# Attention loop on one core: product with the values and output projection one step later, every step's probabilities turned by VectorE through DRAM

## The chip, the cores and the metric

One NeuronCore of one Trainium2 chip. The metric is the device time of one execution in microseconds (us); the runs of the kernel before gave a median of 1366.54 us over three (1366.28 to 1366.75). Lower is better. The engines are called here by the profile's short names: PE is TensorE (PEld its weight loads), DVE is VectorE, ACT is ScalarE, POOL is GpSimd, SP is SyncE, which in this kernel issues all the copies to and from DRAM of the attention loop. Each engine works through its own instructions strictly in program order and is held to the others by semaphores.

## What is computed

Layernorm, cross attention, layernorm, and a mixture of experts with a shared expert, all in float32, over 2048 tokens (32 sequences of 64) of width 512. Only the attention matters here. Cut from the reference:

```
q = rmsnorm(layernorm(x) @ Wq.T, q_norm_w)        # 32 heads of 128
k = rmsnorm(ctx @ Wk.T, k_norm_w)                 # 8 groups of 128, each serves 4 heads
v = ctx @ Wv.T                                    # 8 groups of 128
scores = q @ k.T / sqrt(128) + mask               # 64 x 64 for each sequence and head
out = softmax(scores) @ v
x = x + tanh(g_xattn) * (out @ Wo.T)
```

## The kernel before

The matrix products of float32 data are made of three products of parts: each operand is split in a high part, rounded by ACT, and a low part, the rest, which DVE subtracts; `split_product` (L675 to L679) multiplies high by low, low by high and high by high.

Stage 1 (to about 187 us) makes keys, values and layernormed rows and puts keys and values in DRAM (`kbuf`, `vbuf`). Stage 2 is the attention loop, to about 1040 us. Stage 3 is the mixture of experts and the final sum; the change doesn't touch stages 1 and 3.

The attention loop has STEPS = 64 steps: 8 key groups, and in each NC = 8 steps of 256 tokens (4 sequences). A step has two halves of 128 tokens. What is done for the data of step j, in its order:

- `q_head` (L746) on PE: the queries of two heads per half, 24 matmuls with 512 columns; ACT copies them (`q_out`, L1226, to `qs`) and squares them (`squares`, L1231, to `sq`).
- The sum of the squares: DVE turns the squares by 32x32 blocks and sums them (`turn_squares`, `sum_squares`, `split_sums`), PE finishes the sum with one small matmul (`add_quarters`, L773, into `ps2`), DVE reads it (L1667, L1672), POOL makes the inverse root (`inverse_root`, L566, to `qr`).
- `scores` (L755) on PE, queries by keys (`kt`, one buffer, which holds the keys of two steps): it waits for `kt_in`, that is for the four loads of `load_k` (L363), one of which fills 32 partitions.
- `softmax` (L1656) on DVE, with the exponential on ACT (`exps`): scale, mask, maximum, difference, sum, reciprocal, product. It ends with `p_ready`; the probabilities are in `pb`, one buffer. Into its waits other work is put (`while_root`, `while_exp`).
- The probabilities turned, keys in the partitions. For odd steps: `transpose_probs` (L787) on PE, four transposes, then ACT and DVE split them out of `ps2` and `ps3` (`probs_hi`, `probs_lo`). For even steps 4 to 54 (`BY_DMA`): DVE turns 32x32 blocks (L1738, `pb` to `pbT`, one buffer), SP stores them to DRAM (L419, `pbuf`) and loads them back with blocks exchanged (`probs_back`, L441, four loads to `pt_raw`), and ACT and DVE split `pt_raw` in `pth` and `ptl`.
- `probs_v` (L796) on PE, the product with the values, 24 small matmuls; ACT and DVE split the result (`a_hi_tile`, `a_rest`). POOL splits the values (`split_v`, L570).
- `project_out` (L778) on PE, the output projection, 24 matmuls with 512 columns, in two halves; DVE adds each to the sum in SBUF (`add_out`, L1618).

Within one PE step i (`step`, L843) stand, in this order: the queries of step i + 1, in an odd step the transposes of step i in their midst, the product with the values of step i - 1, the scores of step i + 1, and the output projections behind it (`outputs`, L828): second half of step i - 2, first half of step i - 1. The DVE step (`dve_step`, L1732), the ACT step (`act_step`, L1275) and SP's `next_loads` (L413) follow the same count. In `next_loads` the four loads of `load_k` stand in the odd step i, and there nothing waits ahead of them but `s_done`, which says that the scores that still read `kt` are done:

```
if odd:
    sp.wait_ge(s_done, i + 1)
    load_k(d + 1)
```

The last eight steps (from 56) are written without the turning of the squares and with PE transposes for even steps too. SP's loop over steps 4 to 55 is a hardware loop; the other engines' steps are written out, POOL's are a loop.

## Time and profile before

| | us |
|---|---|
| median of three runs | 1366.54 |
| the profiled execution | 1367.91 |
| its span, first to last instruction | 1366.2 |
| what lies around the span | 1.7 |
| PE busy | 1351.8 (99%) |
| DVE busy | 1041.6 (76%) |
| ACT busy | 505.4 (37%) |
| POOL busy | 359.9 (26%) |

The profiled execution took 1367.91 us and its trace spans 1366.2 us of it; it is 1.4 us (0.1%) above the median of the runs. Busy time counts instructions that compute, not waits. Matmuls are pipelined: each is busy until its result is out, so two that follow each other overlap in the records, and the distance of their starts (0.23 us for 512 columns here) is what one costs, not its duration of 0.39 us. PE is at its granted clock of 2.4 GHz (1.00 in the rows) in all of the loop.

### The profile page before, as it was taken

What the parts mean: (1) busy time and instruction counts of PE and PEld (TensorE: products, weight loads), DVE (VectorE), ACT (ScalarE), POOL (GpSimd) and SP (SyncE); (2) the same over time, 40 slices, a digit from 0 to 9 for tenths busy, and PEclk for the clock granted to TensorE, in tenths of its full rate; (3) what the DMA queues carried; (4) which work ended last, traced back from release to release, by engine and by line L of the source; (5) the groups of instructions that cost most, each with busy time, mean ns of one, the idle gap of its engine ahead of it and who ended that gap; (6) DMA issues with size and microseconds to landing.
All of it is one profiled execution on the core that took longest, in us unless ns stands there. A gap on an engine that the chain in (4) does not pass through costs nothing.

```text
span 1366.2 us, 24589 instructions
## 1 busy us (share of the span) xinstructions
PE 1351.8 (99%) x8473; PEld 1092.8 (80%) x8474; DVE 1041.6 (76%) x2190; ACT 505.4 (37%) x1085; POOL 359.9 (26%) x375
## 2 busy tenths in 40 slices
PE   8999999999999999999999999999999999999998
PEld 7888877888888888888888888888887888777777
DVE  6676668898888888898988888888687655334459
ACT  4233244343434444344334343434344321222242
POOL 1122232212121221212121212122112100467746
PEclk9999999999999999999999999999999999999999
DMA  6766631222122221222121222212222344555548
GB/s 208 248 190 204 187 112 40 59 56 72 50 57 66 62 59 47 76 53 59 50 78 48 59 63 66 55 51 59 55 78 85 132 171 161 193 185 162 168 158 297
DMA packets 178209, 146.13 MB, mean 107 GB/s; under 512 B 77376, under 2 KB 139328, under 8 KB 177856
## 3 DMA queue, kind: packets, MB, share of 16 engines
q1 hardware_dynamic: 170592, 120.17, 29.4%
q0 software_dynamic: 7520, 24.65, 5.4%
q8 instruction: 63, 1.03, 0.3%
q14 instruction: 34, 0.28, 0.1%
HBM read 97.06 MB, written 47.71 MB: 106 GB/s over the span
## 4 chain that ended last, share of the span: by engine, by line
PE 80%; DVE 3%; issue 1%; DMA 0%; ACT 0%; POOL 0%; DVEq 0%; ACTq 0%
PE ps L677 20%; PE ps L679 19%; PE ps L678 19%; PE ps L1071 6%; PE ps L761 5%; PE ps L808 4%; PE ps L1087 3%; PE ps L1066 2%; PE ps L793 1%; DVE acc L2086 1%; DVE acc L2093 1%; PE ps L984 1%; PE ps L816 0%; PE ps L1118 0%; PE ps L769 0%
## 5 line engine op out<-in xcount | busy, mean ns | idle before, releaser
L574 POOL CAST vth<-vt 128x256 fp32r<-128x256 f32 x64 | 25.4, 397 | 538.6 <-PE ps L808 536.6
L1268 ACT CAST ah<-ps 128x256 fp32r<-128x256 f32 x256 | 83.1, 381 | 208.4 <-PE ps L679 202.0
L677 PE MATMUL ps<-hT,w0h 128*128 128x512 f32 x384 | 152.2, 396 | 1.2 <-DVE w0l L1542 1.2
L679 PE MATMUL ps<-hT,w0h 128*128 128x512 f32 x384 | 149.8, 390 | 0.0
L678 PE MATMUL ps<-hT,w0l 128*128 128x512 f32 x384 | 149.6, 390 | 0.0
L568 POOL TENSOR_TENSOR qr<-qv,mhalf 128x8 f32<-128x8 f32 x64 | 105.1, 1642 | 139.2 <-DVE qv L1672 113.5
L1228 ACT ACTIVATE qs<-ps,wqk 128x512 f32<-128x512 f32 x128 | 88.2, 689 | 125.8 <-PE ps L679 125.8
L1623 DVE TENSOR_TENSOR acc<-ps,acc 128x512 f32<-128x512 f32 x128 | 88.0, 687 | 50.5 <-PE ps L679 50.3
L677 PE MATMUL ps<-w0l,ah 128*128 128x512 f32 x256 | 105.9, 414 | 0.0
L1241 ACT ACTIVATE pb<-pb 128x256 f32<-128x256 f32 x128 | 48.3, 419 | 154.4 <-DVE pb L1692 154.4
L677 PE MATMUL ps<-w1l,ah 128*128 128x512 f32 x256 | 105.1, 411 | 0.0
L1629 DVE TENSOR_TENSOR al<-ps,ah 128x256 fp32r<-128x256 f32 x256 | 95.7, 416 | 10.4 <-ACT ah L1268 10.4
L677 PE MATMUL ps<-hT,w1h 128*128 128x512 f32 x256 | 101.2, 395 | 0.0
L679 PE MATMUL ps<-w0h,ah 128*128 128x512 f32 x256 | 100.3, 392 | 0.0
L679 PE MATMUL ps<-w1h,ah 128*128 128x512 f32 x256 | 100.2, 391 | 0.0
L678 PE MATMUL ps<-w1h,al 128*128 128x512 f32 x256 | 99.9, 390 | 0.0
L678 PE MATMUL ps<-w0h,al 128*128 128x512 f32 x256 | 99.9, 390 | 0.0
L679 PE MATMUL ps<-hT,w1h 128*128 128x512 f32 x256 | 99.9, 390 | 0.0
L678 PE MATMUL ps<-hT,w1l 128*128 128x512 f32 x256 | 99.7, 389 | 0.0
L1071 PE MATMUL ps<-wgu,xgT 128*128 x376 | 94.9, 382 | 0.2 <-issue 0.2
L1638 DVE STREAM_TRANSPOSE sqT<-sq 128x512 f32<-128x512 f32 x108 | 75.5, 699 | 20.7 <-ACT sq L1236 20.6
L677 PEld LDWEIGHTS ps<-hT,w0h 128*128 128x128 f32 x384 | 72.1, 188 | 16.7 <-DVE w0l L1542 1.4
(255 smaller groups left out, 3172.8 us busy)
## 6 DMA issues: line engine op xcount, KB each, us to landing
wraw<-in_w_att SPq DMA_DIRECT2D x64, 256.0 KB, 2.7
vbuf<-vo SPq DMA_DIRECT2D x16, 512.0 KB, 3.3
kbuf<-ko SPq DMA_DIRECT2D x16, 512.0 KB, 5.3
kt<-kbuf SPq DMA_DIRECT2D x128, 64.0 KB, 2.2
vt<-vbuf SPq DMA_DIRECT2D x64, 128.0 KB, 2.2
wgu<-in_w_gu SPq DMA_DIRECT2D x4, 2048.0 KB, 7.9
y<-ybuf SPq DMA_DIRECT2D x16, 512.0 KB, 6.9
pbuf<-pbT SPq DMA_DIRECT2D x26, 256.0 KB, 2.0
```

What stands on the lines that cost most here:

```text
L568: pool.tensor_tensor(qr[:], qv[:], mhalf[:, 0:8], ALU.pow).then_inc(q_rt, 1)
L677: pe.matmul(dst, l_hi, r_lo, start=first, stop=False)
L678: pe.matmul(dst, l_lo, r_hi, start=False, stop=False)
L679: return pe.matmul(dst, l_hi, r_hi, start=False, stop=last)
L761: mm = pe.matmul(PS[3][h * S:(h + 1) * S, b * S:(b + 1) * S], qs[:, h, b], kt[:, b, :], start=True, stop=True)
L808: mm = pe.matmul(PS[4 + b2][:, bp * 256:(bp + 1) * 256], vhl[v_part][rows, bp, :], pt[p_part][rows, 2 * part + bp, :], start=(z == 0), sto ...
L1071: mm = pe.matmul(PS[2 + q][:, 0:2 * EI], xgT[q][:, k, :], wgu[:, bass.ds(e, 1), k * 2 * EI:(k + 1) * 2 * EI].rearrange("p a n -> p (a n)") ...
L1228: act.activation(qs[:, h].rearrange("p b s -> p (b s)"), PS[h][:], ACT.Copy, scale=wqk[:, 0:1]).then_inc(q_copy, 1)
L1268: act.copy(ah[:, bp, :, b2, :], pv_view(bp, b2)).then_inc(a_hi, 1)
L1623: dve.tensor_tensor(dst, PS[6 + bp][:], dst, ALU.add).then_inc(acc_done, 1)
L1629: dve.tensor_tensor(al[:, bp, :, b2, :], pv_view(bp, b2), ah[:, bp, :, b2, :], ALU.subtract).then_inc(a_lo, 1)
L1638: dve.transpose(sqT[:].rearrange("p n i -> p (n i)"), sq[:, h].rearrange("p b s -> p (b s)")).then_inc(sq_turned, 1)
```

## The change

The constants `BY_DMA` and `TURNED` move, so that the probabilities of all steps from 2 to 56, odd ones too, are turned by DVE and go through DRAM; PE's transposes remain for steps 0, 1 and 57 to 63. To give the way through DRAM its time, step i of PE now takes the product with the values of step i - 2 (before i - 1), and the output projection behind it the second half of step i - 3 and the first of step i - 2. ACT's and DVE's steps follow, POOL splits the values of step j - 2 ahead of the root of step j, and `catch_up` at step 56 does two steps' products, after which the last steps run as before. SP's order is written anew: probabilities out, keys (odd steps), weights' slice, probabilities back, values. The line numbers in the two kernels differ. The core of the diff:

```
 NC = T // CT
 CB = CT // S
 STEPS = KVH * NC
-BY_DMA = (4, STEPS - NC)
-TURNED = (3, STEPS - NC + 1)
+BY_DMA = (2, STEPS - NC + 1)
+TURNED = (4, STEPS - NC + 1)
...
+        def by_dma(i):
+            return BY_DMA[0] <= i < BY_DMA[1]
+        def pT_before(i):
+            return i if i < BY_DMA[0] else i - (BY_DMA[1] - BY_DMA[0])
+        def att(r):
+            return W[r // NC % 2]
+        def raw_view(x_, odd):
+            return pt[x_][:, :, odd * P:odd * P + P].rearrange("p m (q i) -> p q m i", q=4)
...
+            def load_v(j):
+                sp.wait_ge(v_split, 2 * j)
+                sp.dma_start(vt[:].rearrange("p b t -> p (b t)"), vbuf[j]).then_inc(vt_in, 16)
+            def load_slice(i):
                 sp.wait_ge(w_hi, i + 8)
                 sp.wait_ge(w_lo, i + 8)
                 sp.dma_start(wraw[:], w_att[i + NC]).then_inc(wr_in, 16)
+            def probs_out(i):
+                sp.wait_ge(p_turned, i - BY_DMA[0] + 1)
+                if i > BY_DMA[0]:
+                    sp.wait_ge(p_back, 64 * (i - BY_DMA[0]))
+                sp.dma_start(pbuf, pbT[:].rearrange("p c m i -> p c (m i)")).then_inc(p_out, 16)
+            def probs_back(i):
+                sp.wait_ge(p_out, 16 * (i - BY_DMA[0] + 1))
+                sp.wait_ge(pT_evac, 2 * i)
+                for c in range(4):
+                    sp.dma_start(pt_raw[32 * c:32 * c + 32].rearrange("p q m i -> p q (m i)"),
+                                 p_ld[c]).then_inc(p_back, 16)
+            for i in range(STEPS - NC + 1):
+                if by_dma(i):
+                    probs_out(i)
+                if i % 2:
+                    sp.wait_ge(s_done, i + 1)
+                    load_k(i // 2 + 1)
+                if i == 0:
+                    load_v(1)
+                if i % 2 or not by_dma(i):
+                    load_slice(i)
+                if by_dma(i):
+                    probs_back(i)
+                    load_v(i)
+                if i % 2 == 0 and by_dma(i):
+                    load_slice(i)
+            load_v(STEPS - NC + 1)
...
-            split_v(2)
-            with pool.Fori(3, STEPS - 2) as j:
+            inverse_root(3)
+            with pool.Fori(4, STEPS - NC + 2) as j:
+                split_v(j - 2)
+                inverse_root(j)
+            split_v(STEPS - NC)
+            split_v(STEPS - NC + 1)
+            for j in range(STEPS - NC + 2, STEPS - 2):
                 inverse_root(j)
                 split_v(j)
...
+            def projected_0(r, w_o):
                 pe.wait_ge(a_hi, 4 * r + 6)
                 pe.wait_ge(a_lo, 4 * r + 6)
                 pe.wait_ge(acc_done, 2 * r + 2)
                 project_out(0, w_o, (0, 1, 2, 3))
+            def outputs(r, w_before, w_o, o_ready=None):
+                pe.wait_ge(acc_done, 2 * r + 1)
+                project_out(1, w_before, (0, 1, 2, 3))
+                if o_ready is not None:
+                    pe.wait_ge(w_lo, o_ready)
+                pe.wait_ge(pT_evac, 2 * r + 4)
+                projected_0(r, w_o)
+            def next_query(i):
+                if i % NC == NC - 1:
+                    pe.wait_ge(w_lo, i + 5)
+                for h in range(2):
+                    pe.wait_ge(q_sq, 2 * i + 1 + h)
+                    q_head(h, (i + 1) % 2, (i + 1) % NC // 2, att(i + 1)).then_inc(q_done, 1)
+            def step(i):
+                next_query(i)
+                probs_v(i - 2, i % 2)
+                scores((i + 1) // 2, (i + 1) % 2)
+                pe.wait_ge(acc_done, 2 * (i - 2) + 1)
+                project_out(1, att(i - 3), (0, 1))
+                if i + 1 == TURNED[0]:
+                    pe.wait_ge(const_dve, 6)
+                add_quarters(i + 1)
+                project_out(1, att(i - 3), (2, 3))
+                if i % NC == 2:
+                    pe.wait_ge(w_lo, i + 6)
+                projected_0(i - 2, att(i - 2))
+            def catch_up(i):
+                next_query(i)
+                probs_v(i - 2, 0)
+                scores((i + 1) // 2, (i + 1) % 2)
+                q_sums(i + 1)
+                pe.wait_ge(acc_done, 2 * (i - 2) + 1)
+                project_out(1, att(i - 3), (0, 1, 2, 3))
+                projected_0(i - 2, att(i - 2))
+                probs_v(i - 1, 1)
+                pe.wait_ge(acc_done, 2 * (i - 1) + 1)
+                project_out(1, att(i - 2), (0, 1, 2, 3))
+                projected_0(i - 1, att(i - 1))
...
                 project_out(0, W[0], (0, 1, 2, 3))
-                probs_v(1, 1)
                 pe.wait_ge(s_scaled, 3)
                 pe.wait_ge(ss_turned, 3)
                 scores(1, 1)
-                pe.wait_ge(const_dve, 6)
-                pe.wait_ge(acc_done, 4)
-                transpose_probs(2, 0)
-                outputs(1, W[0], W[0])
-                step(1, 1, 2, W[0], W[0], W[0])
+                q_sums(3)
+            opening()
+            for i in range(3, STEPS - NC):
+                step(i)
+            catch_up(STEPS - NC)
+            for i in range(STEPS - NC + 1, STEPS - 1):
+                last_step(i, o_ready=STEPS if i == STEPS - NC + 1 else None, last=(i == STEPS - 2))
...
+            def probs_hi(i, odd, bank=2):
+                if by_dma(i):
+                    act.wait_ge(p_back, 64 * (i - BY_DMA[0] + 1))
+                    act.wait_ge(pv_done, 2 * i + 2 - 2 * odd)
+                    act.copy(raw_view(0, odd), pt_raw[:]).then_inc(pT_hi, 2)
+            def queries(i):
+                act.wait_ge(s_done, i + 1)
+                for h in range(2):
+                    q_out(h, i + 1)
+                    squares(h, i + 1)
+            def act_step(i):
+                queries(i)
+                a_hi_tile(i - 2, 0)
+                if i % 2:
+                    probs_hi(i - 1, 0)
+                a_hi_tile(i - 2, 1)
+                split_slice(i, att(i + NC), i % NC)
+                if i % 2:
+                    probs_hi(i, 1)
+                exps(i + 1)
+            def act_catch_up(i):
+                queries(i)
+                a_hi_tile(i - 2, 0)
+                a_hi_tile(i - 2, 1)
+                split_slice(i, att(i + NC), i % NC)
+                exps(i + 1)
+                a_hi_tile(i - 1, 0)
+                a_hi_tile(i - 1, 1)
+                probs_hi(i, 0)
...
             def probs_lo(i, odd, bank=2):
-                if odd:
+                if by_dma(i):
+                    dve.wait_ge(pT_hi, 2 * i + 2)
+                    dve.tensor_tensor(raw_view(1, odd), pt_raw[:], raw_view(0, odd), ALU.subtract).then_inc(pT_evac, 2)
...
+            def turn_probs(i):
+                dve.wait_ge(p_ready, 2 * i + 2)
+                if i > BY_DMA[0]:
+                    dve.wait_ge(p_out, 16 * (i - BY_DMA[0]))
+                dve.transpose(pbT[:].rearrange("p c m i -> p (c m i)"),
+                              pb[:].rearrange("p (m z) (h j) -> p (z h) m j", z=2, h=2)).then_inc(p_turned, 1)
+            def dve_step(i):
+                odd = i % 2
+                late = i % 2 == 1 and 3 < i < STEPS - NC - 1
+                turn_probs(i)
+                turn_squares(i + 1, 0)
+                sum_squares(i + 1, 0)
+                if odd:
+                    slice_lo(i - 1, att(i + NC), i % NC - 1)
+                turn_squares(i + 1, 1)
+                sum_squares(i + 1, 1)
+                split_sums(i + 1)
+                a_rest(i - 2, 0)
+                def while_root():
+                    if odd:
+                        probs_lo(i - 1, 0)
+                    elif i > 4:
+                        slice_lo(i - 1, att(i - 1 + NC), (i - 1) % NC)
+                    add_out(2 * i - 3, 1, (2 * i - 5) % NT)
+                    a_rest(i - 2, 1)
+                def while_exp():
+                    add_out(2 * i - 2, 0, (2 * i - 4) % NT)
+                softmax(i + 1, while_root, while_exp, turn_before=i - BY_DMA[0] + 1)
                 if odd:
                     probs_lo(i, 1)
+                    if not late:
+                        slice_lo(i, att(i + NC), i % NC)
+            def dve_catch_up(i):
+                turn_probs(i)
+                a_rest(i - 2, 0)
+                def while_root():
+                    add_out(2 * i - 3, 1, (2 * i - 5) % NT)
+                    a_rest(i - 2, 1)
+                def while_exp():
+                    add_out(2 * i - 2, 0, (2 * i - 4) % NT)
+                softmax(i + 1, while_root, while_exp, turn_before=i - BY_DMA[0] + 1)
+                slice_lo(i, att(i + NC), i % NC)
+                a_rest(i - 1, 0)
+                add_out(2 * i - 1, 1, (2 * i - 3) % NT)
+                a_rest(i - 1, 1)
+                probs_lo(i, 0)
+                add_out(2 * i, 0, (2 * i - 2) % NT)
...
+                turn_probs(2)
+                softmax(3, lambda: None, lambda: None, turn_before=1)
+            opening()
+            for i in range(3, STEPS - NC):
+                dve_step(i)```

How the order on the queues moves. `pbuf`, `pt_raw`, `pbT` are the buffers of the way through DRAM, `kt` the keys, `wraw` a slice of the weights, `vt` the values.

SP, the loads of one odd step before (the last rows of the loop over two steps; the ISA rows make addresses and hold the wait):

```order
L439 DMA vt<-vbuf 128x256
L421 REGISTER_ALU
L365 ISA [waits s_done]
L365 DMA kt<-kbuf 32x16x32
L365 ISA
```

and SP, one odd step of the change:

```order
L430 DMA pbuf<-pbT 128x512 [waits p_back,p_turned]
L369 DMA kt<-kbuf 32x16x32 [waits s_done]
L369 DMA kt<-kbuf 32x16x32 x3
L424 DMA wraw<-in_w_att 128x512 [waits w_lo,w_hi]
L436 DMA pt_raw<-pbuf 32x4x128 [waits pT_evac,p_out]
L436 DMA pt_raw<-pbuf 32x4x128 x3
L419 DMA vt<-vbuf 128x256 [waits v_split]
```

The key loads of an odd step stood behind the values' load of the even step and now stand behind a store that waits for `p_turned`, DVE's turned probabilities of the same odd step.

DVE, the end of one step's softmax and the head of the next step, which is odd, before:

```order
L1701 TENSOR_TENSOR pb<-pb,rc 128x256
L1711 TENSOR_TENSOR ptl<-pt_raw,pth 128x4x4x32 [waits pT_hi]
L1638 STREAM_TRANSPOSE sqT<-sq 128x512 [waits q_sq,sq_sums]
L1707 TENSOR_TENSOR ptl<-ps2,pth 128x2x128 [waits pT_hi]
L1707 TENSOR_TENSOR ptl<-ps3,pth 128x2x128 [waits pT_hi]
L1644 TENSOR_REDUCE sqs<-sqT 128x8x2 [waits sq_turned]
L1720 TENSOR_TENSOR w1l<-wraw,w1h 128x512 [waits w_hi]
```

and of the change:

```order
L1742 TENSOR_TENSOR pb<-pb,rc 128x256
L1775 STREAM_TRANSPOSE pbT<-pb 128x512 [waits p_out,p_ready]
L1679 STREAM_TRANSPOSE sqT<-sq 128x512 [waits q_sq,sq_sums]
L1685 TENSOR_REDUCE sqs<-sqT 128x8x2 [waits sq_turned]
L1759 TENSOR_TENSOR w1l<-wraw,w1h 128x512 [waits w_hi]
```

The turning of the probabilities comes directly behind the softmax's last product; the splitting of even and odd probabilities has moved behind the next reading of `ps2` and behind the next softmax.

PE, in the queries of an odd step before (the four transposes between two heads' parts):

```order
L679 MATMUL ps1<-hT,w0h 128x512
L793 MATMUL ps2<-ident,pb 128x128 [waits p_ready]
L793 MATMUL ps3<-ident,pb 128x128
L793 MATMUL ps2<-ident,pb 128x128 [waits p_ready]
L793 MATMUL ps3<-ident,pb 128x128
L677 MATMUL ps1<-hT,w0h 128x512
```

and the scores in every step of the change, which are as they were:

```order
L777 MATMUL ps3<-kt,qs 64x64 [waits kt_in,q_copy]
L777 MATMUL ps3<-kt,qs 64x64 x15
```

The transposes are gone from the odd steps 3 to 55 and from steps 2 and 56; nothing takes their place on PE.

## Rows read from the trace of the kernel before

**Rows 1.** The page's busy time, share of the span, and instructions, by engine.

```profile
PE 1351.8 (99%) x8473; PEld 1092.8 (80%) x8474; DVE 1041.6 (76%) x2190; ACT 505.4 (37%) x1085; POOL 359.9 (26%) x375
```

**Rows 2.** Stretch 250 to 930 us: busy us of each engine (instructions), PEclk, DMA share, GB/s.

```profile
250.00:930.00 680.00, 680.00 (x4815) 555.18 (x4814) 602.67 (x1315) 271.79 (x630) 140.27 (x153) 1.00 0.23 60
```

**Rows 3.** Waits of PE after 14 us, engine, line, releaser: in total, times, longest us.

```profile
PE ps L761 <- ACT qs L1228: 2.7, 3, 1.0
PE ps L677 <- DVE w0l L1542: 1.2, 1, 1.2
```

**Rows 4.** PE's timeline, steps 23 to 25: start us, us, line, operation, tiles, count.

```profile
508.32 1.15 PE L761 MATMUL ps<-kt,qs 128*64 128x64 f32 x32
509.40 0.50 PE L677 MATMUL ps<-w0l,ah 128*128 128x512 f32 x1
...
510.89 0.19 PE L775 MATMUL ps<-sqs_hl,fold 128*128 128x64 f32 x1
...
515.11 0.39 PE L677 MATMUL ps<-hT,w1h 128*128 128x512 f32 x1
...
520.64 0.38 PE L808 MATMUL ps<-ptl,vth 64*128 64x256 f32 x2
...
521.54 1.15 PE L761 MATMUL ps<-kt,qs 128*64 128x64 f32 x32
...
535.25 1.15 PE L761 MATMUL ps<-kt,qs 128*64 128x64 f32 x32
```

**Rows 5.** DVE's timeline of the same steps.

```profile
506.53 0.76 DVE L1707 TENSOR_TENSOR ptl<-ps,pth 128x256 fp32r<-128x256 f32 x2
...
518.25 0.76 DVE L1701 TENSOR_TENSOR pb<-pb,rc 128x256 f32<-128x256 f32 x2
518.93 0.68 DVE L1720 TENSOR_TENSOR w1l<-wraw,w1h 128x512 fp32r<-128x512 f32 x1
519.53 0.70 DVE L1738 STREAM_TRANSPOSE pbT<-pb 128x512 f32<-128x512 f32 x1
...
523.72 0.19 DVE L1654 TENSOR_TENSOR sqs_hl<-sqs,sqs_hl 128x32 fp32r<-128x32 f32 x1
...
532.15 0.68 DVE L1711 TENSOR_TENSOR ptl<-pt_raw,pth 128x512 fp32r<-128x512 f32 x1
```

**Rows 6.** SP's timeline, the opening's key loads and those for step 26.

```profile
226.21 2.02 SPq L365 DMA_DIRECT2D kt<-kbuf  x4
...
520.36 0.33 SPq L419 DMA_DIRECT2D pbuf<-pbT  x1
...
525.08 1.92 SPq L365 DMA_DIRECT2D kt<-kbuf  x4
```

**Rows 7.** Copies by line, KB each, median us from issue to landing.

```profile
kt<-kbuf SPq DMA_DIRECT2D x128, 64.0 KB, 2.2
...
pbuf<-pbT SPq DMA_DIRECT2D x26, 256.0 KB, 2.0
pt_raw<-pbuf SPq DMA_DIRECT2D x104, 64.0 KB, 1.9
```

**Rows 8.** ACT's timeline, the exponential of step 25.

```profile
529.71 0.76 ACT L1241 ACTIVATE pb<-pb 128x256 f32<-128x256 f32 x2 [2.21 <-DVE pb L1692]
```

**Rows 9.** PE's timeline and windows at the program's start, with PE's clock.

```profile
7.16 0.47 PE L677 MATMUL ps<-w0l,c_hi 128*128 128x512 f32 x1 [1.16 <-DVE w0l L1531]
...
10.03 0.50 PE L677 MATMUL ps<-w0l,c_hi 128*128 128x512 f32 x1 [1.94 <-DVE w0l L1531]
...
10.60:15.00 4.40, 4.40 (x14) 3.45 (x13) 3.23 (x5) 3.10 (x5) 0.00 (x0) 0.61 1.03 415
```

**Rows 10.** PE's timeline, scores of steps 1, 3 and 4.

```profile
202.77 1.15 PE L761 MATMUL ps<-kt,qs 128*64 128x64 f32 x32 [0.98 <-ACT qs L1228]
...
224.34 1.15 PE L761 MATMUL ps<-kt,qs 128*64 128x64 f32 x32
...
238.88 1.15 PE L761 MATMUL ps<-kt,qs 128*64 128x64 f32 x32
```

More of the change, by code:

```diff
@@ L841, in outputs @@
                 project_out(0, w_o, (0, 1, 2, 3))
-            def step(d, odd, pair_q, w_q, w_before, w_o, q_ready=None, o_ready=None, last=False, turn=True):
-                i = 2 * d + odd
-                if q_ready is not None:
-                    pe.wait_ge(w_lo, q_ready)
+            def outputs(r, w_before, w_o, o_ready=None):
[5 more added lines that the diff above has]
+                projected_0(r, w_o)
@@ L869, in step @@
                     transpose_h2(3, 1)
-                dma = turn and by_dma(i, odd)
-                if not odd and not dma:
+                if i % 2 == 0:
                     pe.wait_ge(acc_done, 2 * i)
-                    transpose_probs(i, odd)
-                outputs(i - 1, w_before, w_o, o_ready, turn, dma)
+                    transpose_probs(i, 0)
+                outputs(i - 1, att(i - 2), att(i - 1), o_ready)
             for k in range(KD):
@@ L1284, in act_step @@
                 a_hi_tile(i - 1, 0)
-                if not odd and not by_dma(i, odd):
+                if i % 2 == 0:
                     probs_hi(i, 0)
                 a_hi_tile(i - 1, 1)
-                if by_dma(i, odd) and False:
-                    probs_hi(i, 0, d=d)
-                split_slice(i, w, sl)
-                if by_dma(i, odd):
-                    probs_hi(i, 0, d=d)
+                split_slice(i, W[0], i % NC)
                 exps(i + 1)
-            def act_group(d0, p, t0=0):
-                for t in range(t0, NC // 2):
-                    for odd in range(2):
-                        act_step(d0 + t, odd, W[1 - p], 2 * t + odd)
             act.wait_ge(s_done, 1)
@@ L1751, in dve_step, with dve_last @@
+            def dve_last(i, complete=(None, None)):
+                odd = i % 2
+                if odd:
+                    probs_lo(i, 1)
                 if complete[0] is not None:
```

200 lines of the change are left out of this document (44 added, 156 removed).

## Prediction

> **What bounds the kernel now.** I read the busy times first: PE is busy 99% of the span [rows 1]. The windows by stage show that the attention loop is wholly PE's: 680.0 us of 680 at the full clock, with DVE at 602.7 [rows 2]. The waits confirm it: after 14 us the longest wait of PE is 1.2 us, and none recurs in the loop [rows 3]. So in the loop a matmul taken away is time gained, as long as nothing new makes PE wait. PE's timeline gives the price: the scores of steps 24, 25 and 26 start at 508.32, 521.54 and 535.25 [rows 4]. The first distance is 13.22 us, without transposes in it; the second, 13.71, holds the four transposes of step 25. Four transposes therefore cost PE **0.49 us**. I write S for the start of a step's scores.
>
> **The change part by part.**
>
> *PE's transposes.* They go in the odd steps 3 to 55 and in steps 2 and 56. After the scores of step 4 that is 26 odd steps, 26 x 0.49 = 12.7 us, and 0.5 for step 56. Steps 2 and 3 are in the opening, below.
>
> *DVE.* In an odd step it gains a turning of 0.70 and a split from the loaded copy of 0.68 and loses the pair of 0.76 [rows 5]: 0.62 us more per two steps. Its idle time in the loop is 680 - 602.7 = 77.3 us over 680 / 26.93 = 25.3 pairs, 3.1 us a pair [rows 2]. The pair shrinks by 0.49, so 3.1 - 0.6 - 0.5 = 2.0 us stay: cost nothing, PE's matmuls cover it. Without that cover it would be 0.6 us a pair. The finest margin is `add_quarters`: DVE's split ends at 523.91, and two steps earlier PE's product started 2.57 us after S, which here is 524.11 [rows 4, 5]. The turning before it starts at once behind the softmax, in front of other work that had waited there, and the work moved behind the reading of `ps2` fills DVE's wait for the projection. I take no cost; an upper bound comes with a rival.
>
> *ACT and POOL.* Same instructions, other places; both have more idle than busy time [rows 1]: nothing.
>
> *The later product.* PE's probabilities now have a step more, so the DRAM way of store (2.0 us) and load (1.9 us) [rows 7] is no wait for PE. Instead PE owes one step's product with the values (520.64 to 521.54, 0.9 us) and projection (509.40 to 515.11, 5.7 us) [rows 4] once the loop is full, and pays it at step 56: **+6.6 us**, unless the opening gives it back.
>
> *The key loads, the term that decides.* SP's order of an odd step i is now: store of the turned probabilities of step i, then the four key loads, and these keys are for the scores of step i + 1, in PE's same step i. Before, they were issued at 525.08, some 10 us ahead of the scores at 535.25 [rows 4, 6]. Now the queue of SP stands at the wait for `p_turned`, and behind it wait keys, weights' slice, returned probabilities and values; who waits for the keys is PE, with all that follows. For i = 25: S(25) = 521.54; the softmax's last product leaves DVE at 532.15, where now the turning starts [rows 5]; it ends 0.70 later, 532.85. SP issued the store 0.13 after such an end (520.23 to 520.36) [rows 5, 6]: 532.98. The first key load follows after the store's own 0.33 and a little: 533.36. Four of them, outside SP's hardware loop, took 2.02, so the last starts about 1.69 later [rows 6]: 535.05. It lands after 2.2 [rows 7]: 537.25, and PE starts about 0.1 later, 537.35. Without the wait S(26) would stand at 521.54 + 13.22 = 534.76. The wait is **2.6 us**, once in each odd step. Bounds: with 0.35 between issues and 2.0 to landing, 2.0 us; with the loads delayed behind the store's 256 KB, 3.4 us. I take 2.6, as all its pieces are rows of the same copies. For steps 5 to 55: 26 x 2.6 = 67.6 us. The wait doesn't shorten the next chain, since that starts at S(i + 2), 13.22 us behind.
>
> The Trainium skill has a formula for a copy (DMA: Bandwidth & Descriptors, Anatomy of one DMA): about 2.0 us fixed plus the bytes at 436 GB/s. By it a key load would take 2.15 us, and the wait would be 0.05 smaller, 1.3 us in sum; the trace has 2.0 us for the store of 256 KB, for which the formula gives 2.6, so I keep the rows.
>
> *The opening.* The scores of step 3 move forward by the 0.9 us of a product with the values, 224.34 - 0.9 = 223.44 [rows 10]. The same chain with the key loads, 13.22 + 2.6 = 15.8, puts S(4) at 239.3 against 238.88: +0.4 us. PE has only some 8 us of work there and so stands still for over 7.
>
> *PE's clock.* At the start of the program PE idled for 1.16 and 1.94 us with three matmuls between; behind it the granted clock fell from 2.4 to 1.2 GHz, and the stretch 10.6 to 15.0 has a mean of 0.61 [rows 9]: 4.4 x 0.39 = 1.7 us lost. A gap of 0.98 us in dense work was followed by no fall [rows 10, 2]. The new gap of 2.6 us lies beyond both single gaps, but in dense work. Cost of a fall 0 to 1.7 us; I take a fall after half of the 26 gaps, at 1.5 (part of it passes in a gap): 13 x 1.5 = 19.5 us. After the opening's long gap I count one, 1.7 us.
>
> *The sum*, against the profiled execution's 1367.9: -12.7 - 0.5 + 0.4 + 6.6 + 67.6 + 19.5 + 1.7 = +82.6, so 1450.5. The median of the runs was 1.4 us below that execution: **1449 us**.
>
> **The rivals.**
>
> *The keys wait, but the clock never falls in the loop.* For it: every gap has 26 us of dense matmuls around it, and 1 us gaps did nothing. Against: rows 9. It gives 1449 - 19.5 = 1430 us, chance 0.27.
>
> The Trainium skill's TensorE page (TensorE: Matmul & The Clock Gate, Why this matters for your kernels) speaks for this rival: it warns only of gaps between bursts of matmuls that are longer than mine. By that rule the time is 1430. The fall at the start of this trace, after gaps that were shorter, speaks against reading it so.
>
> *The clock falls after every gap.* 26 x 1.7 = 44.2 in place of 19.5: 1474 us, chance 0.13.
>
> *A second wait, for the returned probabilities of odd steps.* Their loads can't be issued before the even ones are split, behind DVE's reading of `ps2`. From S on: about 4.3 to the first issue, 1.7 to the last, 1.9 to landing [rows 6, 7], 0.6 for ACT's copy: 8.5, where the exponential started at 529.71 - 521.54 = 8.17 [rows 4, 8]. The softmax ends some 0.3 later, inside a margin of about 0.5 before `add_quarters` is late. If landing takes 0.7 longer, PE loses 0.5 per pair: 26 x 0.5 = 13, so 1462 us, chance 0.09.
>
> *The keys come in time* (the other side). One mechanism: the probabilities are turned early enough that the first key load is issued before S(i) + 13.22 - (1.7 + 2.2 + 0.1) = S(i) + 9.2, and my chain has it at S(i) + 11.8. The softmax alone ends at S + 10.6 in the rows, so the order on SP or the wait itself would have to be other than I read it. Then only the transposes count, and filling and emptying the pipeline costs about 3 (0 to 6.6, as the opening's shorter PE work is hidden by DVE or not): 1367.9 - 13.2 + 3 - 1.4 = 1356 us, chance 0.07. About the same time as before, by whatever balance: 0.01.
>
> **How the numbers follow.** The forecast, keys late and a clock that falls after part of the gaps, has 0.43; with the rivals' 0.27, 0.13, 0.09, 0.07 and 0.01 that makes 1. The lower end: no falls, and a wait of 2.0, is 1430 - 15.6 = 1414 us. The upper: a fall after every gap and a wait of 3.0 is 1474 + 10.4 = 1484. What is left out is the case of keys in time and the farther tails. A measurement of this kernel tells about 0.2% from no change, 2.7 us. Faster by more than that: 0.07; within: 0.01; slower: 0.92.
>
> **What would show it.** Right: PE's scores of each odd step (those for even data) wait for the copy to `kt`, 2.0 to 3.4 us, 26 or 27 times, and SP's longest waits are for `pbT`; the scores' distances alternate between 13.2 and about 16 us; no transposes of `pb` on PE between 240 and the last eight steps; PE's mean clock in the loop is below 1.00. PE at 1.00 throughout would show the clock's term wrong; distances of 13.2 us alone, the whole forecast; waits of `add_quarters` for the split sums, that the margin on DVE was smaller than I read it.

## The result, and the profile after

The changed kernel takes **1488.8 us** (1488.2 to 1491.1, 4 runs), the kernel before 1366.4 us (1365.6 to 1366.8, 4 runs) beside it: a ratio of 1.090, 95% interval 1.088 to 1.092. The forecast was 1449, with 1414 to 1484 as its range. So the direction was right and the size was not, and the time lies just above the range.

The busy time by engine, as in [rows 1]:

```profile
PE 1386.6 (93%) x8364; PEld 1119.3 (75%) x8365; DVE 1060.7 (71%) x2186; ACT 505.0 (34%) x1058; POOL 380.1 (26%) x375
```

PE has 109 matmuls fewer and yet 35 us more of busy time, and it idles for 101 us of a span of 1487.3. The window of the loop, with the columns of [rows 2], shows both halves of this: PE stands still for 65 of 680 us, and where it runs its clock is not whole any more.

```profile
250.00:930.00 680.00, 614.67 (x4067) 500.51 (x4065) 537.83 (x1135) 235.04 (x522) 135.89 (x131) 0.94 0.25 68
```

What PE waits for, after 14 us (columns of [rows 3]):

```profile
PE ps L777 <- DMA kt<-kbuf: 85.6, 27, 8.0
PE ps L777 <- ACT qs L1255: 2.7, 3, 1.0
PE ps L693 <- issue: 1.2, 1, 1.2
PE ps L693 <- DVE w0l L1583: 1.2, 1, 1.2
```

The first line is new. One of its 27 waits, 7.96 us, is in the opening; the other 26 are in the odd steps, 77.6 us in total, 3.0 on average (2.50 to 3.54). PE's timeline shows one of them, and what follows (L777 are the scores, the L761 of [rows 4]):

```profile
567.78 1.15 PE L777 MATMUL ps<-kt,qs 128*64 128x64 f32 x32
...
584.48 1.98 PE L777 MATMUL ps<-kt,qs 128*64 128x64 f32 x32 [3.38 <-DMA kt<-kbuf]
586.39 0.80 PE L693 MATMUL ps<-w0l,ah 128*128 128x512 f32 x1
...
588.50 0.48 PE L693 MATMUL ps<-w0l,ah 128*128 128x512 f32 x1
...
599.11 1.15 PE L777 MATMUL ps<-kt,qs 128*64 128x64 f32 x32
```

From 567.78 to 584.48 are 16.70 us, where a step without transposes and without a wait took 13.22. Then the 32 matmuls of the scores take 1.98 us for 1.15, and a product takes 0.80 for 0.48. The windows of the gap and of what follows give the clock (PEclk is the column behind POOL's count):

```profile
578.00:582.50 4.50, 3.10 (x22) 2.27 (x20) 4.09 (x8) 2.98 (x7) 1.12 (x2) 1.00 0.42 99
584.50:586.00 1.50, 1.50 (x29) 1.50 (x30) 0.00 (x0) 0.00 (x0) 0.00 (x0) 0.50 0.00 0
587.90:599.11 11.21, 11.21 (x59) 9.03 (x57) 9.84 (x20) 4.50 (x10) 2.02 (x1) 1.00 0.18 52
```

Behind the gap the granted clock is at 1.2 GHz, and from 587.90 at the latest it is at 2.4 again. In the loop 23 of the 26 gaps have such a fall; seven of these last twice as long. The three without one are the shortest gaps of the loop, 2.50, 2.54 and 2.59 us. Toward the end of the loop one has it and the next has not, which PE's timeline shows by the length of the scores:

```profile
956.99 1.98 PE L777 MATMUL ps<-kt,qs 128*64 128x64 f32 x32 [3.13 <-DMA kt<-kbuf]
973.02 1.15 PE L777 MATMUL ps<-kt,qs 128*64 128x64 f32 x32
988.86 1.15 PE L777 MATMUL ps<-kt,qs 128*64 128x64 f32 x32 [2.54 <-DMA kt<-kbuf]
1002.11 1.15 PE L777 MATMUL ps<-kt,qs 128*64 128x64 f32 x32
```

From 956.99 to 973.02 are 16.03 us, a distance with a long fall; from 988.86 to 1002.11 are 13.25, one without.

**Who holds the keys.** DVE's timeline of step 25, and SP's of the same step (S(25) is 567.78):

```profile
577.78 0.76 DVE L1742 TENSOR_TENSOR pb<-pb,rc 128x256 f32<-128x256 f32 x2
578.58 0.71 DVE L1775 STREAM_TRANSPOSE pbT<-pb 128x512 f32<-128x512 f32 x1
```

```profile
579.32 0.32 SPq L430 DMA_DIRECT2D pbuf<-pbT  x1
579.69 2.10 SPq L369 DMA_DIRECT2D kt<-kbuf  x4
581.88 0.43 SPq L424 DMA_DIRECT2D wraw<-in_w_att  x1
```

The turning begins at S + 10.80, the store goes out 0.03 behind its end, and the four key loads run behind the store, as forecast. In place of the 525.08 of [rows 6], which is 3.54 behind the S of its step, their first is 11.91 behind it. SP's waits from 250 to 1060 us, and the landings:

```profile
SPq L430 <- DVE pbT L1775: 293.0, 52, 7.0
```

```profile
pbuf<-pbT SPq DMA_DIRECT2D x55, 256.0 KB, 2.0
pt_raw<-pbuf SPq DMA_DIRECT2D x220, 64.0 KB, 2.0
kt<-kbuf SPq DMA_DIRECT2D x128, 64.0 KB, 2.4
```

The store lands in 2.0 us as before; the key load takes 2.4 where [rows 7] have 2.2. PE waits for the last of the four, and that one takes 2.6 on average in the odd steps, at most 3.1.

**The account,** from the starts of the scores. S(4) is 239.45, +0.57 to before. From S(4) to S(57) are 826.5 us, before 713.6: +112.9. In it the 26 distances that end at scores of even data grew from 13.71 to a mean of 16.33, which is -0.49 for the transposes, 12.7 us in sum, and +3.11 for the wait (3.0 of it recorded as PE's idle time), 80.7 us in sum; the other 27 grew from 13.22 to a mean of 14.88, 44.9 us in sum, for the clock. From S(57) to S(58) are 22.24 us for 14.53: +7.7. Together +121.1, which is the difference of the two spans, 1487.3 and 1366.2.

### The profile page after: what moved, and what is told of

Its sections match the earlier page's. It is cut to its first block, busy times and chain, and to the rows that moved or that the text cites. A ratio compares the mean times of both kernels' runs of the same rounds, so it can differ in the third digit from the quotient of the medians.

```text
span 1487.3 us, 23913 instructions
## 1 busy us (share of the span) xinstructions
PE 1386.6 (93%) x8364; PEld 1119.3 (75%) x8365; DVE 1060.7 (71%) x2186; ACT 505.0 (34%) x1058; POOL 380.1 (26%) x375
## 4 chain that ended last, share of the span: by engine, by line
PE 57%; DVE 13%; DMA 6%; SPq 3%; issue 3%; POOL 1%; ACT 0%; DVEq 0%; POOLq 0%; ACTq 0%
PE ps L693 13%; PE ps L694 12%; PE ps L695 12%; PE ps L1098 6%; PE ps L777 5%; DMA kt<-kbuf 5%; PE ps L1114 3%; SPq L369 3%; DVE acc L1664 2%; PE ps L824 2%; PE ps L1093 1%; DVE pb L1733 1%; DVE pbT L1775 1%; DVE pb L1727 1%; DVE mx L1730 1%
## 5 line engine op out<-in xcount | busy, mean ns | idle before, releaser
L579 POOL TENSOR_TENSOR qr<-qv,mhalf 128x8 f32<-128x8 f32 x64 | 124.7, 1949 | 265.5 <-DVE qv L1713 233.5
L777 PE MATMUL ps<-kt,qs 128*64 128x64 f32 x2048 | 88.1, 250 | 88.8 <-DMA kt<-kbuf 85.6
L585 POOL CAST vth<-vt 128x256 fp32r<-128x256 f32 x64 | 25.7, 402 | 513.7 <-PE ps L824 511.8
L777 PEld LDWEIGHTS ps<-kt,qs 128*64 128x64 f32 x2048 | 79.1, 161 | 99.5 <-issue 93.4
L693 PE MATMUL ps<-hT,w0h 128*128 128x512 f32 x384 | 151.0, 393 | 1.2 <-DVE w0l L1583 1.2
L1255 ACT ACTIVATE qs<-ps,wqk 128x512 f32<-128x512 f32 x128 | 88.1, 688 | 142.5 <-PE ps L695 142.2
L693 PE MATMUL ps<-w0l,ah 128*128 128x512 f32 x256 | 113.6, 444 | 1.2 <-issue 1.2
L693 PE MATMUL ps<-w1l,ah 128*128 128x512 f32 x256 | 111.8, 437 | 0.0
L694 PE MATMUL ps<-w0h,al 128*128 128x512 f32 x256 | 106.1, 415 | 0.0
L694 PE MATMUL ps<-w1h,al 128*128 128x512 f32 x256 | 105.3, 411 | 0.0
L695 PE MATMUL ps<-w0h,ah 128*128 128x512 f32 x256 | 105.1, 411 | 0.0
L695 PE MATMUL ps<-w1h,ah 128*128 128x512 f32 x256 | 104.7, 409 | 0.0
L693 PE MATMUL ps<-hT,w1h 128*128 128x512 f32 x256 | 100.0, 390 | 0.0
L1708 DVE SCALAR_TENSOR_TENSOR ssg<-ps,quarters 128x64 f32<-128x64 f32 x53 | 14.7, 278 | 115.0 <-PE ps L791 115.0
## 6 DMA issues: line engine op xcount, KB each, us to landing
wraw<-in_w_att SPq DMA_DIRECT2D x64, 256.0 KB, 2.8
pbuf<-pbT SPq DMA_DIRECT2D x55, 256.0 KB, 2.0
```

What stands on the lines that cost most here:

```text
L579: pool.tensor_tensor(qr[:], qv[:], mhalf[:, 0:8], ALU.pow).then_inc(q_rt, 1)
L693: pe.matmul(dst, l_hi, r_lo, start=first, stop=False)
L694: pe.matmul(dst, l_lo, r_hi, start=False, stop=False)
L695: return pe.matmul(dst, l_hi, r_hi, start=False, stop=last)
L777: mm = pe.matmul(PS[3][h * S:(h + 1) * S, b * S:(b + 1) * S], qs[:, h, b], kt[:, b, :], start=True, stop=True)
L1255: act.activation(qs[:, h].rearrange("p b s -> p (b s)"), PS[h][:], ACT.Copy, scale=wqk[:, 0:1]).then_inc(q_copy, 1)
```

## The experiments

Each edit is made in the changed kernel unless said otherwise, and measured beside the kernel before.

### The order on SP, undone

```diff
             for i in range(STEPS - NC + 1):
-                if by_dma(i):
-                    probs_out(i)
                 if i % 2:
                     sp.wait_ge(s_done, i + 1)
                     load_k(i // 2 + 1)
+                if by_dma(i):
+                    probs_out(i)
```

> Edit: in SP's odd steps the four key loads are issued ahead of the store of the turned probabilities instead of behind it; nothing else. Theory K (the whole loss is the key loads that stand behind the wait for DVE's turned probabilities, and the clock that falls in the gaps they make): the waits of PE for kt vanish, the distances of the scores are 13.2 us in every step, PE's clock in the loop is 1.00, and the time is 1352 to 1362 us, faster than before. Rival R (the way of the odd steps' probabilities through DRAM, or DVE's added work, costs of its own): waits of PE for split probabilities, for the split sums or for DVE take the place of those for kt, and the time stays above 1375 us.

Measured: **1364.6 us** (1361.7 to 1366.8, 10 runs), ratio to before 0.998 (0.997 to 0.999): the waits and the clock are as expected, the time is 2.6 us above the range. PE's waits from 190 to 1000 us, and the window:

```profile
PE ps L777 <- ACT qs L1255: 6.8, 4, 4.1
PE ps L693 <- issue: 1.2, 1, 1.2
PE ps L791 <- DVE sqs_hl L1695: 0.4, 1, 0.4
PE ps L824 <- DVE ptl L1747: 0.2, 1, 0.2
```

```profile
250.00:930.00 680.00, 679.46 (x4791) 552.75 (x4790) 631.91 (x1332) 276.13 (x616) 161.81 (x155) 1.00 0.30 80
```

No wait for keys, and no fall of the clock in the loop. The edit takes off 124 us, where the change had cost 122: two lines of order on one queue are the whole loss. The rest of the change is worth some 2 to 3 us, of which the scores' distances give this account. The transposes are -12.7 us. Filling and emptying the longer pipeline is +6.8: 7.7 from S(57) to S(58), less 3.15 by which S(4) is earlier, plus 2.2 from S(4) to S(5), where the clock falls behind the 4.10 us of the first row. Small delays in the loop are +2.9: its distances are 13.3 to 13.6 in a dozen places instead of 13.23.

### What the clock costs, with the wait kept

PE fills the gap with twelve matmuls, written where the scores come to stand and overwritten by them. They start when the scores of the step before have been read.

```diff
+            def fill(i):
+                pe.wait_ge(s_scaled, i + 1)
+                for z in range(12):
+                    k = z % KD
+                    pe.matmul(PS[3][:], att(i + 1)[0][:, k * 512:k * 512 + P],
+                              hT[:, bass.ds(2 * ((i + 1) % NC // 2), 2), 0, k, :], start=True, stop=True)
...
                 probs_v(i - 2, i % 2)
+                if i % 2:
+                    fill(i)
                 scores((i + 1) // 2, (i + 1) % 2)
```

> Edit: the change, with 12 matmuls of 512 columns, whose result is overwritten, put on PE in every odd step of the loop ahead of the scores, where it otherwise waits some 3 us for the keys. Theory K with the clock as a second term (1.7 us per pair of steps, 45 us in all): 12 x 0.227 = 2.7 us of the gap are filled, the clock stays at 1.00, the wait for kt shrinks to 0.3 to 0.6 us, and the time is 1440 to 1450 us although PE does 325 matmuls more. Rival C (the longer even steps come from something else that is late after the gap, not from the clock): the time stays at 1485 to 1495 us.

Measured: **1448.8 us** (1447.7 to 1449.8, 4 runs). PE's timeline:

```profile
520.54 1.15 PE L777 MATMUL ps<-kt,qs 128*64 128x64 f32 x32
537.13 1.15 PE L777 MATMUL ps<-kt,qs 128*64 128x64 f32 x32 [0.31 <-DMA kt<-kbuf]
550.37 1.15 PE L777 MATMUL ps<-kt,qs 128*64 128x64 f32 x32
```

The distance with the gap in it is still 16.59 us, 16.46 on average: the keys come no sooner. But the other distance is 13.24, and the loop has no fall. The clock's share is 1488.8 - 1448.8 = **40 us**, a little less than the 44.9 of the distances, as the matmuls themselves put 0.13 us on each distance with a gap, 3.4 us in sum. The other 82 us above the kernel before are the wait, less the transposes, and the 7.7 of emptying the pipeline. This kernel does 324 matmuls more, and is 40 us faster for it.

The same with six matmuls:

> Edit: the change, with 6 instead of 12 overwritten matmuls ahead of the scores in odd steps: the idle gap shrinks from 3.1 to about 1.7 us. Gaps of 1.0 us were followed by no fall of the clock, gaps of 2.3 us by a fall in 20 of 26 steps, gaps of 3.0 by a fall in 23 of 26. If the clock depends on the length of the gap, between a few and 20 falls are seen and the time lies between 1449 (no fall) and 1482 us; if any gap beyond 1 us does it, over 20 falls and about 1485.

Measured: **1444.7 us** (1443.6 to 1445.7, 2 runs). PE's waits from 250 to 1000 us:

```profile
PE ps L777 <- DMA kt<-kbuf: 32.0, 25, 2.0
```

Gaps of 1.3 us on average, and one fall in the loop, at a gap of 1.74. Half the filler is enough, and the time is 4 us below the range expected, as the distances with a gap are 16.24 us on average and not 16.46. Two gaps here were longer than the one with the fall, 1.78 and 1.98 us, and had none: the length of a gap alone doesn't settle it.

### The wait alone, in the kernel before

```diff
                 if odd:
                     sp.wait_ge(s_done, i + 1)
+                    sp.wait_ge(p_ready, 2 * i + 2)
                     load_k(d + 1)
```

> Edit: the kernel before, with one wait more on SP: in odd steps the key loads are issued only when the probabilities of that step are ready. No other part of the change. Theory K: the softmax ends at S + 10.6, the last of four loads is issued about 1.7 later and lands 2.2 to 2.4 later, S + 14.7, against the 13.7 us distance of an odd step before: a wait of about 1.0 us in each of 31 odd steps, some 30 us, so 1390 to 1405 us, with few falls of the clock or none since the gaps are short. Rival (keys have slack that I don't see, or another load is what PE waits for): 1366 us as before.

Measured: **1410.5 us** (1408.4 to 1412.3, 4 runs), ratio 1.032 (1.031 to 1.034): 5 us above the expectation. PE's timeline, its waits from 250 to 1000 us, and the loop's window:

```profile
513.10 1.15 PE L762 MATMUL ps<-kt,qs 128*64 128x64 f32 x32
528.09 1.15 PE L762 MATMUL ps<-kt,qs 128*64 128x64 f32 x32 [1.21 <-DMA kt<-kbuf]
541.31 1.15 PE L762 MATMUL ps<-kt,qs 128*64 128x64 f32 x32
```

```profile
PE ps L762 <- DMA kt<-kbuf: 27.1, 26, 1.2
```

```profile
250.00:930.00 680.00, 654.68 (x4590) 534.47 (x4589) 581.29 (x1262) 261.05 (x605) 134.22 (x145) 1.00 0.22 57
```

So keys that are tied to the end of the softmax cost time without anything else of the change. With gaps of 1.04 us on average, 26 of them, the clock stays at 2.4 GHz in the loop. Of the 40.5 us by which the span grew, 29 are these distances; 8.2 are the opening, where S(4) is 247.09 for 238.88 and the clock falls once, and some 3 the last steps. The expectation had no term for the opening.

### Only the store taken from ahead of the keys

```diff
-                if by_dma(i):
-                    probs_out(i)
+                if by_dma(i) and i % 2:
+                    sp.wait_ge(p_turned, i - BY_DMA[0] + 1)
                 if i % 2:
                     sp.wait_ge(s_done, i + 1)
                     load_k(i // 2 + 1)
+                if by_dma(i):
+                    probs_out(i)
```

> Edit: in SP's odd steps the key loads still come behind the wait for the turned probabilities, but ahead of the store of 256 KB. Theory K with contention: the wait for the keys shrinks from 3.1 us by the store's 0.37 on the queue and by the landing that its bytes lengthen (2.4 to 3.1 us instead of 2.2), to about 2.2 us; the time falls by 26 x 0.9 = 23 us or a little more, to 1455 to 1470 us. If the order of the two doesn't matter: 1489 us.

Measured: **1461.1 us** (1460.6 to 1461.6, 2 runs). PE's waits from 250 to 1000 us:

```profile
PE ps L779 <- DMA kt<-kbuf: 58.3, 25, 2.9
```

The store itself is worth 28 us: 0.65 us less wait per pair (2.3 for 3.0), and falls at 20 gaps of 26. Most of the 0.65 is the store's place on the queue: the first key load goes out 0.35 us sooner (S + 11.62 for 11.97 on average) and the four 0.18 closer together; their landing got only 0.1 shorter. The falls don't go by length here either: a gap of 1.98 us had one, and one of 2.46 had none. The wait ahead of it is the larger part, as this kernel is still 96 us above the first experiment.

### The slice's bytes taken from beside the keys

```diff
+                if i % 2 and by_dma(i):
+                    sp.wait_ge(kt_in, 64 * (i // 2 + 1) + 64)
                 if i % 2 or not by_dma(i):
                     load_slice(i)
```

> Edit: the change, with the load of the weights' slice in odd steps held back until the four key loads have landed. If the slice's 256 KB, issued 0.2 us behind the last key load, lengthen the keys' landing (2.4 to 3.1 us instead of the 2.2 of the kernel before), the wait for keys shrinks by 0.3 to 0.5 us and the time by 8 to 13 us plus what the clock does. If the store ahead of them is what lengthens it, nothing changes.

Measured: **1478.1 us** (1476.0 to 1480.3, 2 runs), 10.7 us below the changed kernel. PE's waits from 250 to 1000 us, and one of them on its timeline:

```profile
PE ps L779 <- DMA kt<-kbuf: 64.1, 24, 2.9
```

```profile
547.23 1.98 PE L779 MATMUL ps<-kt,qs 128*64 128x64 f32 x32 [2.90 <-DMA kt<-kbuf]
```

The wait is 2.67 us on average, where it was 3.0, and the last key load lands after 2.31 us on average, where it took 2.61. So the 256 KB of the next slice, issued right behind it, had lengthened its landing by 0.3 us. Here all 26 gaps, 2.46 to 2.90 us long, have a fall, and none a double one.

### Taking out the small delays of the loop

Starting from the first experiment. ScalarE's split of odd probabilities stood ahead of the exponentials; where their load came late, the softmax did too.

```diff
                 split_slice(i, att(i + NC), i % NC)
+                exps(i + 1)
                 if i % 2:
                     probs_hi(i, 1)
-                exps(i + 1)
```

> Edit on top of the version with the key loads ahead of the store: in odd steps ACT takes the exponentials first and the returned probabilities behind them, instead of the other way round. That version's scores stand 13.2 us apart in most steps, but 13.3 to 13.6 in some, 5 us in sum over the loop, with DVE waiting there up to 1.0 us for the exponential that waited for the returned probabilities. Theory S (these loads' return is what is late there): all distances become 13.2 us and the time falls by 4 to 5 us, to about 1360. Rival (the small waits are from POOL's slower root or from the weights' slices): at most 1 us is gained.

Measured: **1362.6 us** (1361.0 to 1363.9, 8 runs), ratio 0.997 (0.996 to 0.998). The distances in the loop are 13.23 in nearly every step; the gain is 2 us, half of what was expected. The expectation had counted the 2.2 us behind S(4) among the delays, and those are the clock's; of the 2.9 that are left, 2 are about all there was to win.

With two edits more, one in the opening (ScalarE's first head of the query of step 4 ahead of step 3's exponentials) and one behind the loop (VectorE's `a_rest(i - 1, 0)` ahead of `slice_lo(i)`):

> The version of e6_exp_first, and two edits at the ends of the loop: in the opening ACT copies and squares the first head's queries of step 4 ahead of the exponentials of step 3, so that PE doesn't wait 4.1 us for them; at step 56 DVE splits the product of step 55 ahead of a slice of weights, for which PE waits 1.2 us. Expected if filling and emptying the longer pipeline is the remaining loss: 2 to 3 us less in the opening and 0.6 at step 56, 1357 us. If the opening is bound by DVE's softmax of step 3 anyway, the first edit gives nothing and the time is 1359.

Measured: **1363.3 us** (1362.1 to 1364.2, 9 runs), above both times that were expected and no gain over the last. The edit behind the loop took its 0.6 us (S(57) to S(58) 21.64 for 22.25), but the one in the opening lengthened the distance from step 4 to 5 by 1.0 and won nothing. So the second edit alone:

```diff
                 softmax(i + 1, while_root, while_exp, turn_before=i - BY_DMA[0] + 1)
-                slice_lo(i, att(i + NC), i % NC)
                 a_rest(i - 1, 0)
+                slice_lo(i, att(i + NC), i % NC)
```

> This is e6_exp_first with one more edit, VectorE's a_rest(i - 1, 0) ahead of slice_lo(i) in the two steps behind the loop; the opening stays as in e6_exp_first. In e7_best the same edit took 0.6 us from the distance between the scores of steps 57 and 58 (22.25 to 21.64), while its opening edit lengthened the distance from step 4 to step 5 by 1.0 us. If both readings hold, this kernel is 0.3 to 1 us below e6_exp_first: 1361.5 to 1362.3 us. Rival: the products saved there wait later for something else, and it is equal to e6_exp_first, 1362.6 us.

Measured: **1362.1 us** (1360.7 to 1363.4, 5 runs), ratio to before 0.9956 (0.994 to 0.997), where the kernel before, measured beside it, took 1368.1. Its window, for that of [rows 2]:

```profile
250.00:930.00 680.00, 679.98 (x4768) 554.46 (x4764) 631.92 (x1339) 274.81 (x615) 162.46 (x155) 1.00 0.30 81
```

The 0.6 us are in the distance (21.62); in the time they are within what a run differs by. With the one that takes the exponentials first this is the fastest kernel of the study, some 4 to 6 us below before and 127 us below the change as it was made.

### POOL's root

POOL's `qr<-qv,mhalf` took 1642 ns before. The groups of POOL after:

```profile
L579 POOL TENSOR_TENSOR qr<-qv,mhalf 128x8 f32<-128x8 f32 x64 | 124.7, 1949 | 265.5 <-DVE qv L1713 233.5 <-DVE qv L1704 32.0
```

In the loop it is 2.01 us, 1.64 before. What VectorE does with the root, `pb<-ps,qr`, starts there hardly later, which step 25 shows before (S(25) is 521.54) and after (567.78):

```profile
525.10 1.64 POOL L568 TENSOR_TENSOR qr<-qv,mhalf 128x8 f32<-128x8 f32 x1 [2.08 <-DVE qv L1672]
527.09 0.68 DVE L1681 TENSOR_TENSOR pb<-ps,qr 128x512 f32<-128x512 f32 x1
```

```profile
571.33 2.01 POOL L579 TENSOR_TENSOR qr<-qv,mhalf 128x8 f32<-128x8 f32 x1 [2.07 <-DVE qv L1713]
573.38 0.69 DVE L1722 TENSOR_TENSOR pb<-ps,qr 128x512 f32<-128x512 f32 x1
```

The root ended 0.35 us ahead of VectorE before, which was busy with `al` until then, and ends 0.04 ahead now: VectorE starts at S + 5.60 in place of S + 5.55. So of the 0.37 us only some 0.06 reach the chain. The edit, on top of `exps` first, moves what VectorE does beside the root:

```diff
                 def while_root():
+                    a_rest(i - 2, 1)
                     if odd:
                         probs_lo(i - 1, 0)
                     elif i > 4:
                         slice_lo(i - 1, att(i - 1 + NC), (i - 1) % NC)
                     add_out(2 * i - 3, 1, (2 * i - 5) % NT)
-                    a_rest(i - 2, 1)
```

> POOL's root took 1.64 us in the loop of the kernel before and 2.01 us in the changed one and in e1 and e6. What differs beside it is VectorE's work: before, an addition that reads PSUM; now a subtraction of 512 columns whose two inputs and output lie in SBUF. Here VectorE's a_rest(i - 2, 1), which waits for ScalarE, stands first in while_root, so that the subtraction comes behind the root, or only over its end. Theory that the two disturb each other in SBUF: the root falls to 1.5 to 1.7 us in the loop. Rival, the root is longer for another reason (its place in the program, its own inputs): it stays at 2.0 us. The time of the kernel rises, whichever holds, because VectorE idles for some 1 us a step: 1365 to 1390 us.

Measured: **1404.0 us**, one run, 14 us above the range expected of its time. The loop on POOL and DVE:

```profile
505.99 1.64 POOL L579 TENSOR_TENSOR qr<-qv,mhalf 128x8 f32<-128x8 f32 x1 [2.54 <-DVE qv L1713]
...
515.89 0.40 POOL L585 CAST vth<-vt 128x256 fp32r<-128x256 f32 x1 [8.26 <-PE ps L824]
516.37 0.74 POOL L587 TENSOR_TENSOR vtl<-vt,vth 128x256 fp32r<-128x256 f32 x1
```

```profile
507.74 0.68 DVE L1759 TENSOR_TENSOR w1l<-wraw,w1h 128x512 fp32r<-128x512 f32 x1
...
516.40 1.25 DVE L1759 TENSOR_TENSOR w1l<-wraw,w1h 128x512 fp32r<-128x512 f32 x1
```

The root is back at 1.64 us, in every step of the loop. The second fence shows the same thing from the other side: VectorE's subtraction takes 0.68 us alone and 1.25 where it starts 0.03 behind POOL's. In this run the two subtractions meet 25 times. Fourteen times POOL's started first, by 0.03 to 0.34 us; it took 0.73 us and VectorE's 0.94 to 1.26. Eleven times VectorE's started first or at the same time (within 0.02 us); it took 0.68 us and POOL's 1.09 to 1.30. So the one that starts second pays. The time of the whole rose because VectorE idles 1.1 us before `a_rest` in each step (60.1 us in 53 places), and PE's work on the squares waits for it, which the expectation had priced too low.

## Why the prediction was right or wrong

**In short.** Two terms of the sum were too small. The larger failure is the clock's: 21.2 us were forecast and 44.9 measured. The other is the wait's: 67.6 us, 2.6 each time, were forecast, and 80.7 measured, 3.1 each time.

**Right, the mechanism.** The term that was named as the deciding one decides: SP stands at `p_turned`, the keys wait behind the store, and PE waits for the keys 26 times, once in each odd step, by 2.5 to 3.5 us. The first experiment shows it by taking the cause away. The transposes' 0.49 us is right too: with keys in time and the exponentials first, the distances are 13.23. The margins of DVE, ACT and POOL made no wait for PE of their own in the loop of the changed kernel: all that PE waits for there are the keys.

**Wrong in size: the wait, 2.6 forecast, 3.1 measured.** The miss is 80.7 - 67.6 = 13.1 us. Two pieces of the chain were off. The turning of i = 25 began at S + 10.80, not S + 10.61: POOL's longer root is 0.06 us of that, and most of the rest is that the forecast took the start of VectorE's next instruction (532.15) for the end of the softmax's last product, which ends 0.1 us later and for which the turning waits. As the store then followed sooner, the first key load was 0.15 us later than forecast on average (S + 11.97 for 11.82). The larger piece, 0.4 us, is the landing. It was taken as 2.2, the median of loads with nothing issued close behind them; the last of the four, ahead of a slice of 256 KB, takes 2.6 on average and 3.1 at worst. The slice alone is 0.3 us of it, shown by its experiment. The upper bound of 3.4 did hold the mean; what failed is the choice within the bounds: "all its pieces are rows of the same copies" is no reason, when the same copies now have new neighbours.

The formula of the Trainium skill (DMA: Bandwidth & Descriptors, Anatomy of one DMA — SWDGE (gpsimd) path), about 2.0 us plus the bytes at 436 GB/s, is fitted there to copies that GpSimd issues, and these are SyncE's. The estimate by it is 2.15 us for the key load and 2.6 for the store. The traces have 2.4 in the median, up to 3.1, and 2.0: too low for the one and too high for the other.

**Wrong in size: the clock.** "A fall after half of the 26 gaps, at 1.5" and 1.7 for the opening, 21.2 us in all; it was 44.9 us by the distances, and 40 us by the experiment that fills the gap. There were 23 falls in place of 13, seven of them twice as long. This is the largest miss, 23.7 of the 38.5 us by which the change of the span was above the sum. In the runs, by the mean of the 26 gaps in dense work, gaps of 1.0 us had no fall, of 1.3 us one, of 2.3 us 20, of 2.7 us 26, and of 3.0 us 23. Between means of 1.3 and 2.3 us falls become the rule; single gaps don't follow their length strictly, and what else decides stays open. With the rows 9 and 10 alone this couldn't be placed, and an even chance for 2.6 us was a middle between two unknowns; that all gaps have nearly the same length, so that most will do the same, spoke for one of the ends instead, 1430 or 1474, and against the middle that was made the forecast.

The rival "the clock falls after every gap" had the mechanism almost right (1474, chance 0.13); with the wait as measured it is 1474 + 13.1 = 1487. That its 44.2 us meet the 43.3 measured behind these 26 gaps is in part luck: three gaps had no fall and seven a double one. The rival without a fall, 1430, is refuted: where the slice is held back, all 26 gaps of 2.46 to 2.90 us between stretches of dense matmuls had one. The Trainium skill's page that spoke for this rival (TensorE: Matmul & The Clock Gate, Why this matters for your kernels) warns only of longer gaps; here the measurement decides against it.

**Smaller terms.** Emptying the pipeline was +7.7 for the 6.6 - 0.5 forecast; 1.2 of it is PE standing at the projection of step 56, where the profile names no releaser; that the `a_rest` edit halves it to 0.6 speaks for the rest `al`. The opening was +0.57 for +0.4, in the changed kernel; in the first experiment, with the keys in time there too, it gives back 3.2 us. The second wait, for the returned probabilities, cost the changed kernel nothing that can be seen; with the keys in time it is there, but small: the reordered exponentials win 2 us where the rival had 13. The last rival, keys in time, was priced at 1356; the first experiment is its own test, with 1364.6: 2.9 us for the delays in the loop, and 3.8 more for filling and emptying (6.8 where 3 was put), are most of what was missing.

**The range** ended at 1484 because it took a fall after every gap with a wait of 3.0 as its end, though 3.4 was written down as the bound of the wait. With that bound it would have been 1474 + 26 x 0.8 = 1495, and would have held the time. The wait's lower bound has a slip, on which nothing here depends: 3 x 0.35 us in place of 1.69 and 2.0 in place of 2.2 make 1.8 us of it, not 2.0.

## What to carry to other kernels

A queue is served in order, so ask of every wait that a change writes into it what stands behind it and who needs that first: here a store moved two lines up made 124 us, while the work saved and the work added came out even. Write loads for the bounding engine ahead of stores whose data are needed later. And price a wait of TensorE with what its clock does afterwards: gaps near 3 us cost half as much again in what followed (44.9 to 80.7 us), so one that can't be removed is worth filling with useless matmuls, or shortening to about 1 us.

## What was not expected of the hardware

POOL and VectorE hinder each other in a way that the busy shares don't show. POOL's root of 128x8 takes 1.64 us beside a VectorE operation that reads PSUM and 2.01 beside one whose inputs both lie in SBUF, and VectorE's subtraction takes 0.68 alone and 1.25 beside POOL's. The change makes the longer root the rule in the loop by exchanging what VectorE does while it waits for the root. The kernel before has it once, behind the loop, where VectorE subtracts a slice of weights beside the last root: 2.01 us there too. Only some 0.06 us of the 0.37 reach the chain of the softmax; the rest passes while VectorE is busy with other work. The Trainium skill has the rule (GPSIMD Engine Reference, 1. Specifications): the interfaces to SBUF are shared, with contention when the VectorE instruction has two SBUF inputs. The traces agree, with the times just given. The forecast put POOL at "nothing", which by the chain was nearly right, but without having asked.

The clock falls at gaps of 2 to 3 us amid dense matmuls: at 69 of 78 in the three kernels that have such gaps, and at 1 of 52 in the two with gaps of 1.0 and 1.3 us on average. Matmuls of no use, 12 in each gap of 3 us, made a kernel 40 us faster.
